# Decoder block: q, k and v of the first attention prepared, stored and loaded by token halves

## The reference, cut to what matters

```
def _L0_attn_ref(inputs, qkv_kernel, qkv_bias):
    B, S, E, H = (2, 256, 128, 16)
    b, s, e = inputs.shape
    hidden, heads = (E, H)
    qkv = jnp.einsum('bse,ef->bsf', inputs, qkv_kernel) + qkv_bias
    qkv_heads = qkv.reshape(b, heads, s, -1)
    q, k, v = jnp.split(qkv_heads, 3, axis=-1)
    scale = 1.0 / np.sqrt(2.0 * hidden)
    qk = jnp.einsum('bhse,bhte->bhst', q, k) * scale
    mask = jnp.triu(jnp.full((s, s), -jnp.inf, dtype=jnp.float32), k=1)
    attn = jax.nn.softmax(qk + mask, axis=-1)
    out = jnp.einsum('bhst,bhte->bhse', attn, v).reshape(b, s, e)
    return out
...
x = x + _L0_attn_ref(_layernorm(x, axis=-1), L0_attn_qkv_kernel, L0_attn_qkv_bias)
x = x + _L0_xattn_ref(_layernorm(x, axis=-1), ctx_768, L0_xattn_Wq, L0_xattn_bq, L0_xattn_Wk, L0_xattn_bk, L0_xattn_Wv, L0_xattn_bv)
```

## Time and profile before

| | |
|---|---|
| time, median of 3 runs | 267.82 us (266.85 to 270.07) |
| the profiled execution | 270.48 us, its span 268.4 us |
| mean granted TensorE clock | 0.962 |
| busy share of the span | PE 92%, DVE 66%, ACT 54%, POOL 29% |
| chain that ended last, by engine | PE 64%, DVE 14%, ACT 7%, DMA 6% |
| DMA | 21992 packets, 11.64 MB, 42 GB/s over the span |

### The profile page before, as it was taken

The page is one execution under the profiler, slowest core; times in us unless marked ns, Lnnn a source line. Parts: engine busy times, 40 slices in busy tenths (PEclk is TensorE's granted clock), DMA queues, the critical chain, the costliest instruction groups (busy, mean ns, idle before and its releaser), DMA issues.

```text
span 268.4 us, 5513 instructions
## 1 busy us (share of the span) xinstructions
PE 246.7 (92%) x1995; PEld 170.2 (63%) x1995; DVE 176.5 (66%) x604; ACT 144.3 (54%) x297; POOL 77.3 (29%) x137
## 2 busy tenths in 40 slices
PE   8897899975988999999999798899998999999995
PEld 8553678753654647666665553648896566777775
DVE  4374878657355755485424969487684588889975
ACT  0654576724454577778655235474746754443550
POOL 7667800001010445657674111147331000000000
PEclk9999799998699999999999659999999999999999
DMA  5889920049011000000000000000000000000002
GB/s 138 155 192 298 306 51 4 2 99 292 2 42 39 2 0 2 0 1 2 0 1 4 0 0 0 2 0 5 2 5 0 0 2 0 1 2 0 0 2 78
DMA packets 21992, 11.64 MB, mean 43 GB/s; under 512 B 10969, under 2 KB 20958, under 8 KB 21966
## 3 DMA queue, kind: packets, MB, share of 16 engines
q1 hardware_dynamic: 20925, 10.94, 15.4%
q0 software_dynamic: 80, 0.20, 0.8%
q10 hardware_dynamic: 960, 0.16, 0.3%
HBM read 8.68 MB, written 2.62 MB: 42 GB/s over the span
## 4 chain that ended last, share of the span: by engine, by line
PE 64%; DVE 14%; ACT 7%; DMA 6%; issue 4%; POOL 2%; ACTq 2%; POOLq 0%; DVEq 0%; SPq 0%
PE bank L1035 10%; PE bank L1023 9%; PE bank L912 6%; PE bank L885 4%; PE bank L893 4%; PE bank L652 3%; PE bank L930 2%; PE bank L970 2%; DMA V<-q_scratch 2%; PE bank L789 2%; DMA q_scratch<-QKVT 2%; DVE XN L1719 2%; PE bank L760 2%; POOL rs L445 2%; PE bank L772 1%
## 5 line engine op out<-in xcount | busy, mean ns | idle before, releaser
L445 POOL TENSOR_TENSOR rs<-rs,halves 128x4 f32<-128x4 f32 x14 | 14.4, 1031 | 81.5 <-DVE rs L1712 75.2
L520 POOL TENSOR_TENSOR X<-X,att 128x128 f32<-128x128 f32 x72 | 30.3, 455 | 21.1 <-ACT att L1457 21.1
L1023 PE MATMUL bank<-XT,Wb 128*128 128x512 f32 x64 | 30.0, 600 | 0.7 <-ACT XT L1311 0.7
L1035 PE MATMUL bank<-Wb,att 128*128 128x128 f32 x224 | 27.1, 277 | 0.0
L1035 PEld LDWEIGHTS bank<-Wb,att 128*128 128x128 f32 x224 | 26.1, 192 | 1.4 <-issue 1.4
L1497 ACT ACTIVATE att<-bank 128x512 f32<-128x512 f32 x32 | 18.8, 600 | 8.8 <-PE bank L1023 8.7
L1457 ACT ACTIVATE att<-bank,comb 128x128 f32<-128x128 f32 x72 | 20.4, 377 | 3.6 <-PE bank L912 3.6
L912 PEld LDWEIGHTS bank<-W2a,att 128*128 128x128 f32 x144 | 18.2, 191 | 5.6 <-issue 4.2
L1893 DVE SCALAR_TENSOR_TENSOR att<-bank,cols,att 128x512 f32<-128x512 f32 x18 | 13.5, 749 | 11.6 <-ACT att L1446 7.0
L1719 DVE TENSOR_SCALAR XN<-X,mv,rs 128x128 f32<-128x128 f32 x48 | 14.4, 364 | 9.5 <-POOL rs L445 9.3
L912 PE MATMUL bank<-W2a,att 128*128 128x128 f32 x144 | 19.4, 278 | 0.0
(11 more groups left out here) (232 smaller groups left out, 503.7 us busy)
## 6 DMA issues: line engine op xcount, KB each, us to landing
Wb<-in_L_ffn_W SPq DMA_DIRECT2D x1, 1024.0 KB, 5.2
Wb<-in_L_ffn_W SPq DMA_DIRECT2D x8, 128.0 KB, 5.0
X<-in_x SPq DMA_DIRECT2D x2, 256.0 KB, 3.0
k_scratch<-QKVT SPq DMA_DIRECT2D x1, 512.0 KB, 4.0
q_scratch<-QKVT SPq DMA_DIRECT2D x1, 512.0 KB, 5.0
Wb<-k_scratch SPq DMA_DIRECT2D x1, 512.0 KB, 4.6
v_scratch<-QKVT SPq DMA_DIRECT2D x1, 512.0 KB, 5.8
V<-q_scratch SPq DMA_DIRECT2D x1, 512.0 KB, 6.2
```

The costliest lines, as they stand in the source:

```text
L445: nc.gpsimd.tensor_tensor(rs[:, 0, cut], rs[:, 1, cut], halves[:, :], ALU.pow).then_inc(l_root[h], 1)
L520: nc.gpsimd.tensor_tensor(X[:, h * HT + t, :], X[:, h * HT + t, :], part0[:, i % 2, t, :], ALU.add).then_inc(f_acc, 1)
L1023: mm(bank[i % 4][:, :], W1b[:, e, f * P:(f + 1) * P], XT[:, half(h)], start=True, stop=True).then_inc(m_up, 1)
L1035: last = mm(bank[4 + h][:, t * P:(t + 1) * P], hid[:, e % 2, f, tile], W2b[:, e, f, :], start=(f == 0), stop=(f == F1 - 1))
```

## The change

The round trip of q, k and v is done for half 0 and half 1 apart. `QKVT`, the scratch and the loaded tiles `KH`, `QH`, `VH` are laid out half by half, so that a run in the scratch is 32 numbers (128 bytes) instead of 64. Six stores of 2048 runs take the place of three, and six loads of 128 rows of 2048 bytes that of three with 4096. The early widenings wait for the loads of half 0, and POOL for those of half 1.

To feed this, the normalisation is done half 0 first, then half 1; PE does the three products of half 0 before it transposes half 1; and the orders on PE, ACT and DVE are written anew. `ssm_operands` and the products `keys_values1(2)` and `(3)` move from ahead of the scores into the attention loop. They use bank 7 there, one after the other. POOL's DMAs of the bias `bv0` and the mask `masku` wait for the first half's `XN` instead of the second's, and stand behind `root(0, 1)` as before. The way back of the outputs is as it was. Further on, single calls change places with neighbours, in the rest of the attention loop and the first mixture of experts too.

The core of the diff:

```diff
-        qkv_d = [nc.dram_tensor(f"{name}_scratch", [P, N], fp32).ap() for name in ("q", "k", "v")]
+        qkv_d = [nc.dram_tensor(f"{name}_scratch", [2, P, HALF], fp32).ap() for name in ("q", "k", "v")]
...
-            return 2 + j % 4 if j < 4 else j % 2 if j < 8 else j % 4
+            return (4, 5, 7, 7)[j] if j < 4 else j % 2 if j < 8 else j % 4
...
-            store(1, k_copied, st_k)
-            store(0, q_copied, st_q)
-            load(1, st_k, Wb[:, 0:N], ld_kh)
-            store(2, v_copied, st_v)
-            load(0, st_q, V2[:, :, :].rearrange("p c s -> p (c s)"), ld_qh)
-            load(2, st_v, Wb[:, N:2 * N], ld_vh)
+            def store(s, h, copied, stored):
+                sp.wait_ge(copied, h + 1)
+                sp.dma_start(qkv_d[s][h, :, :].rearrange("(h e) (c x) -> e c h x", e=HD, c=CH).rearrange("e c h x -> (e c) h x"),
+                             QKVT[:, s, half(h)].rearrange("p (h x) -> p h x", h=CH)).then_inc(stored, 16)
+
+            def load(s, h, stored, dst, loaded):
+                sp.wait_ge(stored, 16 * (h + 1))
+                sp.dma_start(dst[:, half(h)], qkv_d[s][h, :, :]).then_inc(loaded, 16)
+
+            store(1, 0, k_copied, st_k)
+            store(0, 0, q_copied, st_q)
+            store(2, 0, v_copied, st_v)
+            load(1, 0, st_k, Wb, ld_kh)
+            load(0, 0, st_q, QL, ld_qh)
+            load(2, 0, st_v, Wb[:, N:2 * N], ld_vh)
+            store(1, 1, k_copied, st_k)
+            store(0, 1, q_copied, st_q)
+            store(2, 1, v_copied, st_v)
+            load(1, 1, st_k, Wb, ld_kh)
+            load(0, 1, st_q, QL, ld_qh)
+            load(2, 1, st_v, Wb[:, N:2 * N], ld_vh)
...
-            pool.wait_ge(ld_kh, 16)
+            pool.wait_ge(ld_kh, 32)
...
-            pool.wait_ge(ld_vh, 16)
-            nc.gpsimd.tensor_copy(VD[:, HB:B, :, :], VH[:, HB:B, :, :]).then_inc(vd_late, 1)
+            pool.wait_ge(ld_vh, 32)
+            nc.gpsimd.tensor_copy(VD[:, HB:B, :, :], VH[1]).then_inc(vd_late, 1)
...
+                if j == 2:
                     pe.wait_ge(pow_ready, 1)
-                    pe.wait_ge(q_copied, 1)
-                    pe.wait_ge(v_copied, 1)
-                    pe.wait_ge(k_copied, 2)
+                if j == 3:
+                    pe.wait_ge(kv_ready, 2)
...
+            bias_rows()
+            projection()
+            copy_xt(0, 0, 0)
+            columns()
+            project(0, 0)
+            project(0, 2)
+            copy_xt(0, 1, 1)
             context(0)
             context(1)
+            project(1, 2)
+            project(1, 0)
+            widen_keys(0)
+            keys_values1(0)
+            widen_keys(1)
+            widen_queries()
             keys0(0)
-            ssm_operands()
-            widen_keys(0)
-            widen_keys(1)
             keys0(1)
-            widen_queries()
-            keys_values1(0)
-            keys_values1(2)
             align_values()
...
+            ln_moments(0, 0)
+            ln_apply(0, 0)
+            ln_moments(0, 1)
+            heads()
+            ln_apply(0, 1)
+            project(0)
+            project(1)
```

More of the change, by code:

```diff
@@ L1080, in prefix @@
                 last.then_inc(r_pre, 1)
+            transpose_xn(0, 0, 0)
+            refill()
+            columns()
+            product(0, 0)
+            product(0, 1)
+            product(0, 2)
+            transpose_xn(0, 1, 1)
             context(0)
+            product(1, 0)
+            product(1, 1)
+            product(1, 2)
             context(1)
-            ssm_operands()
             keys0(0)
             values0(0)
-            keys0(1)
             values0(1)
@@ L1090, in _ @@
             keys_values1(1)
-            keys_values1(2)
-            keys_values1(3)
+            keys0(1)
             scores(0)
@@ L1099, in _ @@
             transpose_probs(2)
+            ssm_operands()
+            keys_values1(2)
+            keys_values1(3)
             weigh_values(0)
@@ L1126, in _ @@
             weigh_values(8)
-            scores(6)
             weigh_values(9)
             transpose_probs(10)
+            scores(6)
+            scores(7)
             transpose_probs(11)
-            scores(7)
+            outputs_by_token(0)
             weigh_values(10)
-            outputs_by_token(0)
+            weigh_values(11)
             transpose_probs(12)
-            weigh_values(11)
             keys_values1(4)
@@ new lines, in bias_rows, with columns, project @@
+            def bias_rows():
+                act.wait_ge(ld_vecs, 128)
+                AF(biases[:, :].rearrange("s (e c) -> s e c", c=CH), vecs[0:3, :].rearrange("s (c e) -> s e c", e=HD),
+                   ACT.Copy).then_inc(c_bias, 1)
+            def columns():
+                act.wait_ge(prep_psum, 1)
+                AF(cols[:, :], bank[4][:, 0:34], ACT.Copy).then_inc(prep_act, 1)
+            def project(h, i):
+                act.wait_ge(prep_act, 1)
+                act.wait_ge(p_psum[h], i + 1)
+                s, copied = ((1, k_copied), (0, q_copied), (2, v_copied))[i]
+                AF(QKVT[:, s, half(h)].rearrange("p (h n t) -> p n h t", h=CH, t=GT),
+                   bank[2 + 3 * h + i][:, :].rearrange("p (n h t) -> p n h t", h=CH, t=GT), ACT.Identity,
+                   bias=cols[:, 31 + s:32 + s]).then_inc(copied, 1)
@@ L1707, in ln_moments @@
             def ln_moments(n, h):
+                if n == 0:
+                    dve.wait_ge(ld_x[h], 16)
                 if n == 3:
@@ L2056, in _ @@
             subtract_max(2)
+            values1(1)
             subtract_max(3)
+            values1(3)
+            inverse(0)
+            inverse(1)
             row_max(4)
-            inverse(0)
-            row_max(5)
-            inverse(1)
             normalise(0)
             normalise(1)
+            row_max(5)
             subtract_max(4)
@@ L2067, in _ @@
             inverse(2)
-            normalise(2)
             row_max(6)
-            inverse(3)
             row_max(7)
             subtract_max(6)
+            row_max(8)
+            normalise(2)
+            inverse(3)
+            normalise(3)
             subtract_max(7)
-            normalise(3)
-            row_max(8)
-            subtract_max(8)
             inverse(4)
@@ L2093, in _ @@
             row_max(12)
+            subtract_max(12)
             normalise(8)
             inverse(9)
-            normalise(9)
             row_max(13)
-            subtract_max(12)
-            row_max(14)
-            inverse(10)
             subtract_max(13)
             add_attention(0)
+            normalise(9)
+            inverse(10)
             ln_moments(1, 0)
-            normalise(10)
+            row_max(14)
             subtract_max(14)
             ln_apply(1, 0)
+            normalise(10)
             row_max(15)
```

220 lines of the change are left out of this document (96 added, 124 removed).

## The result

The changed kernel takes 275.17 us, the median of 4 runs (274.8 to 279.88), against 268.53 for the kernel before (266.85 to 270.07): ratio 1.0244, 95% interval 1.016 to 1.0329. It is slower, and more so than predicted (271.9, range 265.5 to 275.0). The profiled execution took 274.8 us with a span of 272.7, against 270.48 and 268.4 before: 4.3 us more. In all that follows a run more than 1.5% above the fastest of its kernel counts as slow and is left out of the ratios and their intervals, but not out of the medians.

The account below looks back on a forecast made before the run. PE, busy 92%, was taken as the bound through its arrival at transpose_values(1). Late half +2.45 and clock +1.6 gave +4.05 us: profiled 270.5 to 274.5, 1% over the median, hence 271.9 us against median 267.8; range 265.5 to 275.0.

Parts of the forecast that it names:

- Bound at transpose_values(1): Attention loop: PE's arrival at transpose_values(1), 36.95 us before, sets the time; its work from there only shifts.
- The early half: Start: half 0's round trip lets scores(0) start near 23.0, 4 us sooner than 27.07, likely at full clock.
- What eats it in the loop: Loop: keys_values1(2) waits for operand copies; PE reaches transpose_values(1) at 35.9, so 4 us gained shrink to 1.
- The late half: Half 1's round trip and POOL's work: vd_late at 39.4, between 36.9 and 42.4, which transpose_values(1) waits for.
- T: SP's queue: time per half store, taken as 1.9 us at 15 ns a packet, ends 1.5 and 2.34.
- the two ends of the range: Late k's landing: 25.8 at the low end, 31.3 at the high end, around 28.3.
- The sum, clock: transpose_values(1) moves +2.45 us; a low-clock stretch of 3.2 us behind PE's wait adds 1.6; sum +4.05.
- Later edits, 0: Exchanged calls, experts' included, issue the same instructions beside PE's full queue: 0, between -0.6 and +0.6 us.
- Late half in time: Rival at transpose_values(1): T = 1.5, mask's transfer in nobody's way, vd_late at 36.9, 268.3 us; chance 0.18.
- Much too late: Rival in SP's queue: six half stores cost what whole ones do, vd_late 42.4, 274.9 us; chance 0.20.
- Faster by clock: Rival: later low-clock stretches (2.7 and 4.4 us) vanish; one gone gives 268.3, both 264.8; chance 0.12.

Follow-up runs that it names:

- its 128-byte version: Kernel before with each of the three stores issued as two of 128-byte runs, loads and orders kept: 269.18 us, ratio 1.0058.
- its two filler runs: Kernel before with unread PE products ahead of scores(0) and transpose_xn(1,0): 20 and 14 took 271.47 us, 8 and 7 took 268.07 us.
- filler in the loop after: Changed kernel with 28 extra PE products, results unread, in the attention loop's pauses: 273.05 us, ratio 1.0251.
- both moves: Changed kernel with late q and v widened by DVE, and ssm_operands, keys_values1(2), (3) spread behind transpose_values(1): 273.14 us, ratio 1.0188.
- mask first: Changed kernel with POOL's bias and mask transfers issued ahead of root(0, 1): 276.41 us, ratio 1.023.
- DVE: Changed kernel with POOL's last three late instructions (two widenings of q, copy of v) done by DVE: 275.16 us, ratio 1.0241.
- mask first with filler: Changed kernel with POOL's bias and mask transfers ahead of root(0, 1) and 16 unread PE products in loop pauses up to weigh_values(1): 273.71 us, ratio 1.0182.
- filler in the kernel before: Kernel before with unread PE products in two pauses; which amount is not said: 20 and 14 (271.47 us) or 8 and 7 (268.07 us).
- state-space operands early: Changed kernel with ssm_operands, keys_values1(2) and (3) ahead of scores(0) again: 272.44 us, ratio 1.0221.
- all repairs: Last run: changed kernel, DVE widening late q, v; state-space calls behind transpose_values(1); mask's transfer early; before's experts' order; no filler: 270.83 us, ratio 1.0109.

## Why the prediction was wrong, point by point

- **Bound at transpose_values(1).** Right as long as the loop's order is kept: the loop behind it took 14.8 to 14.9 us in every such profile without low clock in it (before, its 128-byte version, its two filler runs, filler in the loop after). It is not a block that only shifts when it starts sooner with more work in it: with both moves it took 20.26 us at full clock, with PE waiting for DVE and ACT.
- **The early half.** Right: 23.02, at full clock (forecast 23.0).
- **What eats it in the loop.** The mechanism was right, keys_values1(2) waits for the operands' copies (1.56 us). The undisturbed time was 0.7 us too early: weigh_values(0) at 35.4 with filler (forecast 34.7). I worked out the pauses and did not ask what they do to the clock. It is low from 33.4 on, and PE is at transpose_values(1) at 38.7, not 35.9. In the run with the mask first the late half is done at 36.7 and PE still comes at 38.77: its own late arrival is enough to keep transpose_values(1) there.
- **The late half.** 39.4 forecast, 39.40 measured, with two errors that cancel. A packet's own time was 15.6 ns, as forecast, but the packets overlap: one passed in 10.5 ns in the early stores and in 13 in the late ones (2461 from 24 to 26 us), so T = 1.35 to 1.7. The trip began later, though. The early k store, issued at 11.23, had its first packets at 14 behind the mask, and the late one, issued at 19.75, had them in number only from 21.75, behind the early loads. I had allowed 1 and 0.5 us for these. The Trainium skill's price per packet (DMA: Bandwidth & Descriptors, section Why small descriptors are slow) is a fixed 3 cycles beside 32 bytes a cycle, which makes 7 against 11; by it the 19.0 ns of before would become 12.1 as an estimate, and the trace agrees roughly, with 10.5 to 13. Two figures in the working don't follow from its own terms: six half stores, not three, stand ahead of the late k's landing, so 11.6 ns a packet would have moved it by 2.6 us and not 1.3; and the two ends of the range start from an issue at 18.6 and 21.2, where the terms give at most 18.3 and 20.8.
- **The sum, clock.** +2.45 was exact. The clock behind it, 1.6, measured 2.09: 4.2 us of the low stretch lay behind transpose_values(1), not 3.2. Of outputs_by_feature(0) I forecast +4.05, and it came out +4.54. That the wait for POOL brings the low clock was wrong for this profile, since the clock fell at 33.4, ahead of that wait: PE's pauses do so alone (mask first, DVE), the wait does so alone (mask first with filler), and only with both filled is it gone.
- **Later edits, 0.** Wrong: the exchanged calls of the experts cost 1.50 us at full clock, undone in four profiles (49.95 to 49.99 against 51.47 to 51.50). They cost 0.4 more in the stage behind it, which takes 70.8 us without low clock in before's order (filler in the kernel before) and 71.2 in after's (state-space operands early). The 1.9 us lie outside the bounds of -0.6 to +0.6 that I gave. Which of the exchanges costs it was not tried apart.
- **The step that failed** is the last of the sum, together with that mis-sized term: "it lies 1% over the median, so against the median 267.8". The forecast is 3.3 us too low, and 2.7 of them are this subtraction. The kernel after does not lie under its profile (median 275.17, profiled 274.8), while the kernel before does, because its profile has more low clock than its usual run. The profiles' difference itself came out as forecast (+4.3 against +4.05), but by terms that cancel: 4.54 in the loop, 1.9 by the experts' order and 1.9 of after's low clock in later stages (1.49 and 0.37), against 4.15 of before's there (2.21 and 1.94), with 0.15 of small ones. A run of before at 0.987 is 3.6 us shorter than its profile, and the median of its four runs 2.0 us (268.53 against 270.48), so half or more of before's 4.15 is missing from the medians, while after's loss is in them.
- **Rivals.** Late half in time: no run reached the 268.3 forecast for it. With it in time and the loop's order kept (mask first) the fastest run took 273.34. Much too late: its time came, its cause didn't; one packet passes in 10.5 ns. Faster by clock: no; the clock moved the other way. The prices were too high as well: before's two later stretches cost 2.2 and 1.9 us, not 2.7 and 4.4.

Left open: even with all repairs 1% remains. In its profile outputs_by_feature(0) is at 56.24, with low clock from 28.9 to 32.4 and from 39 to 46; the run with both moves had no low clock there, and 52.68, with PE waiting for ACT and DVE. No run separates the two. Open too is which pauses bring the low clock. State-space operands early kept 1.00 behind 1.51, 0.69, 0.97 and 0.78 us, the run with both moves kept it behind 0.90, 0.78 and 1.29 us, up to 60.9, and the last run lost it at 28.9 behind 0.83 and 0.78, which the kernel after passes at 1.00.

## What to carry to other kernels

Splitting a transfer to start sooner moves the first half forward and the second half back: look at who consumes the second half, and whether the work that filled the old pause now stands in a full stretch. Price a new pause twice, by its length and by what the same work takes at the lower clock behind it, and look for pauses ahead of the one that you forecast, since the clock can have fallen before. Before a difference of two profiles is set against a median of other runs, compare their mean clocks.

## What the hardware showed that I had not expected

- Stores with 128-byte runs moved 0.39 MB in 2 us and those with 256-byte runs 0.43: one packet in 10.5 ns on each engine against one in 19.0. So half the run cost a tenth of the bandwidth there. SP's issues grew too: 3.44 us for v's two stores in the 128-byte version of the kernel before (0.59 for one before), and 2.55 for early q's store while the mask's transfer ran, but 0.80 with the mask's transfer first.
- At low clock the same work costs differently by stage: 10.2 us of it cost 4.8 in the loop (19.56 against 14.78), 1.9 in the state-space stage (72.72 against 70.8), and 6.8 us cost 2.2 in the cross attention (15.38 against 13.17).
- Once low, the clock stayed so although PE was busy: it was low for 10 us behind the wait of 2.19 us with PE busy for 11.00 of 11 us in that window, and for 7 to 17 us behind the 1.56 us pause in the loop, but for only 3.4 behind before's pause of nearly 2 us.
